# A cross-attention kernel on one Trainium2 core: units of the first attention over three slots, and one pipeline behind the first MLP

## What is computed

```python
# model 0, twice with its own weights: 16 heads of width 128, one bias key and value per head
h = layer_norm(x) * scale + offset
q, k, v = h @ wq + bq, ctx @ wk + bk, ctx @ wv + bv
k, v = concat(k, bias_k), concat(v, bias_v)
x = x + softmax(q k^T / sqrt(128)) v @ wo + bo
# then
x = x + gelu(layer_norm(x) @ w_fc1 + b_fc1) @ w_fc2 + b_fc2        # inner width 1024
# model 1: 16 heads of width 16, keys and values from ctx and from x, ctx masked
h = concat(ctx, x)
k, v = split(h @ kv_w + kv_b);  q = x @ q_w + q_b
y = softmax(mask(q k^T / 16)) v @ out_w + out_b + x
out = gelu_tanh(rmsnorm(y) * w @ mlp_w1 + b1) @ mlp_w2 + b2 + x
```

## Time and profile before

| | us |
|---|---|
| runs | 1424.93, 1425.11, 1517.13 |
| median | 1425.11 |
| the profiled execution | 1426.43 |
| its span, first to last instruction | 1424.7 |
| TensorE busy (matmul) | 1366.2 (96%) |
| DVE busy | 902.9 (63%) |
| ScalarE busy | 620.4 (44%) |
| GpSimd busy | 307.6 (22%) |
| mean granted TensorE clock | 0.983 |

### The profile page before, as it was taken

The page is one execution under the profiler, slowest core; times in us unless marked ns, Lnnn a source line. Parts: engine busy times, 40 slices in busy tenths (PEclk is TensorE's granted clock), DMA queues, the critical chain, the costliest instruction groups (busy, mean ns, idle before and its releaser), DMA issues. The chain is left out here.

```text
span 1424.7 us, 27588 instructions
## 1 busy us (share of the span) xinstructions
PE 1366.2 (96%) x11607; PEld 1219.9 (86%) x11607; DVE 902.9 (63%) x1876; ACT 620.4 (44%) x1022; POOL 307.6 (22%) x290
## 2 busy tenths in 40 slices
PE   5999999999999999999999999998898999997898
PEld 4889998999999898999999999987887877776787
DVE  4866667576666777666666666668534378886322
ACT  4633433434343564334343434346422337775421
POOL 2201011010110112011011010112863023334654
PEclk9999999999999999999999999999999999998999
DMA  5100000001100000000000000000000000002000
GB/s 154 60 31 1 30 11 21 30 1 31 30 2 31 1 31 1 30 31 1 30 1 31 31 2 30 10 22 23 1 1 9 0 2 2 2 3 64 5 30 29
DMA packets 28012, 30.53 MB, mean 21 GB/s; under 512 B 684, under 2 KB 26868, under 8 KB 27892
## 3 DMA queue, kind: packets, MB, share of 16 engines
q1 hardware_dynamic: 27668, 28.72, 6.3%
q10 hardware_dynamic: 226, 0.10, 0.0%
HBM read 26.73 MB, written 2.10 MB: 20 GB/s over the span
## 5 line engine op out<-in xcount | busy, mean ns | idle before, releaser
L334 POOL TENSOR_TENSOR WLO<-W,WHI 128x512 fp32r<-128x512 f32 x64 | 80.7, 1290 | 765.9 <-DVE WHI L728 765.9
L761 DVE STREAM_TRANSPOSE PRT<-PR 32x256 f32<-32x256 f32 x512 | 223.2, 436 | 8.4
L768 DVE TENSOR_TENSOR CLO<-bank,CHI 128x512 fp32r<-128x512 f32 x128 | 88.0, 691 | 145.6 <-ACT CHI L649 145.6
L626 ACT ACTIVATE KT<-bank,PH 128x512 f32<-128x512 f32 x128 | 88.0, 688 | 186.1 <-PE bank L171 186.1
L169 PE MATMUL bank<-WHI,CHI 128*128 128x256 f32 x576 | 167.5, 291 | 0.0
L170 PE MATMUL bank<-WLO,CHI 128*128 128x256 f32 x576 | 161.5, 280 | 0.0
L171 PE MATMUL bank<-WHI,CLO 128*128 128x256 f32 x576 | 161.0, 280 | 0.0
L169 PE MATMUL bank<-WHI,SRC_HI 128*128 128x256 f32 x504 | 146.2, 290 | 0.0
L170 PE MATMUL bank<-WLO,SRC_HI 128*128 128x256 f32 x504 | 140.9, 280 | 0.0
L171 PE MATMUL bank<-WHI,SRC_LO 128*128 128x256 f32 x504 | 140.8, 279 | 0.0
L791 DVE TENSOR_TENSOR X<-X,bank 128x512 f32<-128x512 f32 x128 | 88.0, 688 | 68.0 <-PE bank L171 67.4
(11 more groups left out here) (230 smaller groups left out, 3124.2 us busy)
## 6 DMA issues: line engine op xcount, KB each, us to landing
W<-in_wall SPq DMA_DIRECT2D x17, 1024.0 KB, 5.6
W<-in_ctx SPq DMA_DIRECT2D x4, 512.0 KB, 6.8
X<-in_x SPq DMA_DIRECT2D x4, 512.0 KB, 8.6
mlp_w<-in_w SPq DMA_DIRECT2D x2, 1024.0 KB, 9.1
out<-X SPq DMA_DIRECT2D x4, 512.0 KB, 2.9
W<-in_wall SPq DMA_DIRECT2D x1, 512.0 KB, 6.5
W<-in_wall SPq DMA_DIRECT2D x2, 256.0 KB, 8.3
W<-in_qw SPq DMA_DIRECT2D x1, 256.0 KB, 2.8
```

Of the source, the lines that this page charges most:

```text
L334: i = e.tensor_tensor(WLO[a][:, j, :, :], W[a][:, j, :, :], WHI[a][:, j, :, :].bitcast(F32), ALU.subtract)
L626: e.activation(KT[:, h, :, 0:S], PROJ[2 + h][:, :].rearrange("p (q k) -> p q k", k=S), ACT.Identity, bias=PH[:, 1, 2 * pair + h:2 * pair + ...
L761: i = e.transpose(PRT[b * S + z:b * S + z + 32, :, b * S + y:b * S + y + 32], PR[b * S + y:b * S + y + 32, :, z:z + 32])
L768: e.tensor_tensor(CLO[:, h, :], bank[3 + h][:, :], CHI[:, h, :].bitcast(F32), ALU.subtract).then_inc(c_lo, 1)
```

## The change

Three things, all in one diff of 1,500 lines.

**1. The first attention.** A unit goes over three slots. bias_at(n) becomes bias_of(u). TensorE's slot (with the last layer norm's first turn moved in front of output, and the borrowed banks of the bias turns now TB):

```diff
-                        bias, turned_before, turned_now = bias_at(n), apply_at(n - 1), apply_at(n)
+                        bias, turned_before, turned_now = bias_of(n - 1), apply_at(n - 1), apply_at(n)
...
                         keys(n)
+                        if n == 2:
+                            weighted(0)
+                        elif n > 2:
+                            output(n - 2)
...
                         queries(n)
                         values(n, 0)
                         if bias is not None:
...
+                            bias_turns(*bias, (TB[1], TB[0]), n - 1)
+                        if n == 2:
+                            output(0)
-                        weighted(n - 1)
                         values(n, 1)
...
                             norm_turn(e, norm, *turned_now, PROJ)
...
                         scores(n)
-                        output(n - 1)
+                        if n > 1:
+                            weighted(n - 1)
```

ScalarE and DVE:

```diff
                     for n in range(1, SLOTS):
-                        bias, took, now = bias_at(n), stats_at(n), apply_at(n)
+                        bias, took, before = bias_of(n - 1), stats_at(n), apply_at(n - 1)
+                        if n > 2:
+                            weighted_out(n - 2)
+                        exponential(n - 1)
+                        if before is not None:
+                            for c in range(DC):
+                                scale_chunk(e, *before, c, PROJ)
                         keys_out(n)
...
-                        weighted_out(n - 1)
                         values_out(n, 1)
...
                             norm_sqrt(e, norm, *took)
-                        exponential(n)
-                        if now is not None and now[0] < NL:
-                            scale_chunk(e, *now, 1, PROJ)
...
+                        if n >= 2:
+                            weighted_rest(n - 2)
...
                         softmax(n - 1)
...
+                        if n >= 2:
+                            settle(n - 2)
...
-                        weighted_rest(n - 1)
...
                         shifted(n)
-                        settle(n - 1)
```

**2. The way into the first MLP.** TensorE:

```diff
-                    for q in range(4):
-                        up(q)
+                    up(0)
+                    up(1)
+                    output(SLOTS - 2)
+                    up(2)
+                    up(3)
                     e.wait_ge(sub_done, SLOTS)
                     bias_turns(NL - 1, G - 1, (TB[1], None), SLOTS - 1)
                     weighted(SLOTS - 1)
+                    up(4)
                     e.wait_ge(ptb_out, NL * G)
                     norm_turn(e, norm, NL, 1, TB)
+                    up(5)
                     output(SLOTS - 1)
-                    e.wait_ge(fc2_lo, 1)
+                    up(6)
+                    up(7)
                     e.wait_ge(norm.scaled, (NL * G + 2) * DC)
                     norm_turn(e, norm, NL, 2, TB)
-                    for q in range(4, MQ + 4):
+                    e.wait_ge(fc2_lo, 1)
+                    for q in range(4):
+                        down(q)
+                    e.wait_ge(norm.scaled, (NL * G + 3) * DC)
+                    norm_turn(e, norm, NL, 3, TB)
+                    for q in range(8, MQ + 4):
```

```diff
+            def piece_of(s):
+                w, i = window(s)
+                if w == 0:
+                    if i < 4:
+                        return "v", i, 0
+                    j = i - 4
+                elif i < 2:
+                    j = i
+                elif i < 4:
+                    return ("n", w - 2, i - 2) if w >= 2 else None
+                elif i < 10:
+                    j = i - 2
+                elif i < 12:
+                    return "o", w - 1, i - 10
+                else:
+                    j = i - 4
+                g = w + 1
+                if g >= G:
+                    return None
+                if j >= 8:
+                    return "v", g * GT + j - 8, 0
+                return ("x", "kc", "q", "kx")[j // 2], g, j % 2
```

A window w is 16 steps. "x" is one of two turns of a group of x (x_hi on ScalarE, x_lo on DVE), "kc", "kx" and "q" are projections (evacuated by ScalarE), "v" a value tile (three copies on DVE, values_out), "o" two tiles of the output product (sum_y on DVE), "n" a turn of the rms-normed group (normed_out, two activations on ScalarE). TensorE waits ahead of each piece until FILL is free:

```diff
+                    def piece(s):
+                        kind, g, j = piece_of(s)
+                        e.wait_ge(*left_by(s))
...
+                            if s > LT:
+                                e.wait_ge(tl_out, s - LT)
...
+                        if s < STEPS:
+                            piece(s)
+                        elif s < STEPS + 6:
...
+                            up(s - STEPS)
+
+                    e.wait_ge(*left_by(STEPS))
+                    output(G - 1, 0)
+                    up(6)
+                    e.wait_ge(y_sum, 2 * G - 1)
+                    output(G - 1, 1)
+                    up(7)
+                    e.wait_ge(tl_out, STEPS)
+                    normed_turn(2, 0, TURN)
+                    e.wait_ge(y_sum, 2 * G)
+                    normed_turn(2, 1, FILL)
+                    for q in range(4):
+                        down(q)
+                    e.wait_ge(y_scaled, 3 * DC)
+                    for c in range(DC):
+                        normed_turn(3, c, (TURN, FILL)[c])
+                    for q in range(8, MQ + 4):
+                        if q < MQ:
+                            up(q)
+                        down(q - 4)
```

More of the change, by code:

```diff
@@ L665, in _ @@
                     queries_out(0)
-                    for c in range(DC):
-                        scale_chunk(e, 0, 1, c, PROJ)
-                    exponential(0)
                     ctx_round(2)
@@ L1402, in program, with runs @@
+            def runs(s, lag):
+                return 0 <= s - lag < STEPS
             with nc.Block() as block:
@@ L1437, in _ @@
+                    for q in range(4, 8):
+                        gelu(q)
+                    normed_out(2, 0, TURN[:, :])
+                    normed_out(2, 1, FILL[:, :])
+                    root(3)
+                    for c in range(DC):
+                        normed_out(3, c, (TURN, FILL)[c][:, :])
+                    for q in range(8, MQ):
+                        gelu(q)
                 @block.vector
                 def _(e):
-                    e.wait_ge(ob_in, 16)
-                    base(e, 0)
@@ new lines, in _, with x_lo @@
+                    e.tensor_copy(swap[:, S:P], ident[:, 0:S]).then_inc(swap_set, 1)
+                    for half in HALF:
+                        e.tensor_reduce(HM[half, :], ident[half, half].rearrange("p (h d) -> p h d", d=DH), AX_X, ALU.add)
+                    def x_lo(g, c, src):
+                        e.wait_ge(xl_hi, g * DC + c + 1)
+                        toks = slice(g * GTOK, (g + 1) * GTOK)
+                        e.tensor_tensor(SRC_LO[:, 1, c, toks], src, SRC_HI[:, 1, c, toks].bitcast(F32),
+                                        ALU.subtract).then_inc(xl_lo, 1)
@@ new lines, in _ @@
+                    for c in range(DC):
+                        x_lo(0, c, bank[3 + c][:, :])
+                    e.wait_ge(mask_in, 32)
+                    e.wait_ge(ma_set, 1)
+                    for half, row in zip(HALF, mrow):
+                        e.tensor_scalar(MA[half.start:half.start + 1, :, :], row.rearrange("p (b s) -> p b s", s=S),
+                                        0.0, MASKED, ALU.is_equal, ALU.mult).then_inc(ma_set, 1)
+                    e.wait_ge(ow_in, 16)
+                    e.tensor_copy(owh[:, :, :], owr).then_inc(owh_done, 1)
@@ L1483 @@
+                    sum_y(G - 1, 0)
+                    sum_y(G - 1, 1)
+                    normalised(3)
+                    for q in range(4, MQ):
+                        if q % FC == 4 and q > FC:
+                            add(q // FC - 1)
+                        rounded(q)
+                    add(G - 1)
 def kernel(**inputs):
```

1065 lines of the change are left out of this document (535 added, 530 removed).

## The result

The changed kernel takes 1417.46 us in the median of 5 runs (1415.68 to 1420.11), the kernel before 1424.93 to 1429.17 us in four of its five. The ratio is 0.993, 95% interval 0.9912 to 0.9947: 9 to 10 us less, clear of the spread of the runs but within the 2% that the prediction takes for the least that counts as a change. Of 50 runs of the kernel before, beside this and the later kernels, 15 took 1516.9 to 1518.9 us, as one of the three of its first row did, and are left out of the ratios, while none of 50 runs with the one-block pipeline took over 1421; parts12_alone and the kernels behind it show what is likely behind these 90 us.

What follows compares the result with a forecast made beforehand. TensorE was taken as full in the first attention and steps, losing time only at few places and two poor stages; -1.6 - 7.9 - 3.7 - 21.1 + 23.2 = -11.1 us from 1425.11 gave 1414.0 us, range 1390 to 1440.

Steps and rivals of the forecast that it cites:

- likeliest case: Whole kernel: the forecast of 1414.0 us holds, with a time between 1403 and 1425 us; chance 0.54.
- part 5: Second attention's steps: waits and visits charged for 60.7 us of matmuls moved in, +23.2 us (+6 to +50).
- part 4: Behind the steps: last MLP's matmuls fill idle time, leaving a normalisation chain that loses 2.6 us; -21.1 us (-22 to -14).
- rival A: Second attention's steps take all moved work without waits, only visits remain: 1398 us, 1393 with a free start; chance 0.18.
- Part 1: First attention: fewer switches between matmul kinds and fewer waits for queries, against a slower start; -1.6 us (-9 to +6).
- Part 2: End of the first attention: MLP matmuls between the turns fill TensorE's waits; -7.9 us (-9.5 to -4).
- Part 3: From the first MLP to step 0: most projections move into the steps, less is lost; -3.7 us (-7 to 0).
- visits: In the steps: 40 split pieces between float32 work, 0.18 us each to enter and leave, +7.2 us (4 to 12).
- port lock: In the steps: GpSimd's long operations and DVE's SBUF copies block each other on the shared port, +4 us (0 to 24).
- B: Filled steps: the single FILL bank and fixed queue orders make TensorE wait in every one, 1443 us; chance 0.15.
- C: Steps: GpSimd's additions and splits fall on DVE copies in full, +20 us instead of +4, 1430 us; chance 0.13.
- Rival D: First attention: the change there does nothing measurable; held within the forecast, with no chance of its own.

Runs made afterwards that it cites:

- parts12_alone: The changed kernel up to the end of the first MLP, followed by the second model of the kernel before: 1514.6 us.
- mlp0_order: Changed kernel with DVE's normalisation and block roundings, and GpSimd's block remainders, ahead of the second weight's split at the first attention's end: 1411.7 us.
- visits_doubled: Changed kernel with each of the 18 projections in the steps cut into two visits of three matmuls: 1416.9 us.
- short_gpsimd: Changed kernel with three of GpSimd's long operations computed on 16 of 256 columns only, the rest left uncomputed: 1410.8 us.
- root_late: Changed kernel with the third group's root split: squares behind the exponentials of steps 60 to 63, square root and normalisation later: 1406.3 us.
- combined kernel: Changed kernel with root_late, mlp0_order and ScalarE's two scalings ahead of the exponential in slot 1, all together: 1400.5 us.
- middle_filled: parts12_alone with twelve extra 256-column matmuls ahead of the scores in each of steps 28 to 35: 1474.7 us.

## Why the prediction was right

1414.0 us against 1417.5, inside the likeliest case. The likeliest mechanism, the two poor stages filled and the steps longer, is what happened, but its terms missed in both directions and evened out: part 5 by 10 us, part 4 by 8 the other way, parts 1 and 2 by 7 together. So the mechanism was right in the main, and that the total came within 3.5 us is in part luck. Two of its sums do not come out: rival A without the cost of the start is 1396 by its terms, not 1393, and the chain of part 4 leaves 2.3 us and not 2.6. Neither changes the forecast's case.

- **Part 1**: -1.6 forecast, +3.1 measured (the start's 0.4 us not counted). The start cost 3.75 in the profiled execution and 2.5 by the 63.7 of six other kernels, where 2 was forecast, and the wait of 3.9 us came out at 4.22. The slots gave 0.033 us each instead of 0.05 (14.28 for 14.31), 348.52 to 347.72 for 24 of them. The waits in the middle came out as a sum: the two of 0.84 and 1.05 us went and one of 1.25 (at 539.36) came, -0.6, where -2.2 and +1.6 had been set. What the sum did not hold at all is the bias slots: five of them took 0.20 to 0.22 more, and the last slot 0.6. In slot 30, for one, the float32 matmuls stand in three places among the split ones where they had stood in two.
- **Part 2**: -7.9 forecast, -5.6 measured. "Stretched" normalisations were priced at 1 us; they took 2.7 more than undisturbed, and TensorE waited 2.2. mlp0_order gives this back.
- **Part 3**: -3.7 forecast, -4.7 measured.
- **Part 5**: +23.2 forecast, +12.9 measured, the largest miss. The visits were mis-sized, some 4 for 40 pieces instead of 7.2 (and not by the change between kinds of matmul, as visits_doubled shows), the turns of x with the projection behind them some 4 instead of 5.5, weight roundings 0 instead of 3, the port lock about 0 instead of 4 (short_gpsimd). Against that the turns of the rms-normed groups cost 2.4 where 0.8 had been set, and the root of the last window 3.2 in the steps, where it was 2.7. The first four steps gave 1 back.
- **Part 4**: -21.1 forecast, -13.5 measured. Here the step that failed is the clock. The chain behind the steps was worked out at full clock, without the half clock that the idle time of 2.3 us in step 62 brings. With that idle time gone (root_late) the stage and the last MLP give 13.5 + 7.1 = 20.6 us, the forecast's 21.

Of the rivals, A's number (1398) is nearly what the combined kernel reaches (1400.5), by removing waits rather than by there being none. B was refuted by visits_doubled and by the filled steps of 3.5 us, C by short_gpsimd and the unstretched maxima; but four normalisations are stretched wherever they meet GpSimd, and TensorE waits for them at two places. Rival D held, even for parts 1 and 2 together: about nothing in the medians.

The prediction judged the change by the usual execution only. The largest effect of the one-block pipeline is not in the 10 us: in none of 50 runs was it some 90 us longer, as the kernel before was in 15 of 50. That those are steps at half clock is likely from the mean clock and not profiled.

## What to carry to other kernels

Price an idle time of TensorE in front of sparse float32 work by the clock that it may lose behind it, not by its length alone: here 2.3 us cost 10 with what followed, and behind 2.7 us with another 1.3 the steps took 89 us more. A stage of small matmuls that runs at the full clock in one profile can hold the half clock in another kernel with the same steps, so look at the granted clock of every run; in two kernels here, matmuls mixed into eight of the steps brought the clock back. When an operation with a table load moves into a pipeline, put it where the next table load is due anyway, and split off what needs no table.

## What the runs showed of the hardware that was not expected

- The granted clock stayed at 0.50 for 215 us (1160 to 1375) in which TensorE had no gap, in the profile of parts12_alone; its other four runs have the same time and the same mean clock (0.914 to 0.915). It rose to 1.00 within ten us when twelve matmuls of 256 columns were added per step (0.73 in the window 1250 to 1260 of middle_filled).
- The same code can be followed by half clocks of different length: behind step 62 it lasted 10.2 us in three kernels and 20.5 in two, with 24.3 to 25.9 and 29.6 to 29.8 us for the stage.
- Where four normalisations from SBUF met GpSimd's subtractions, they took 4.05, 4.63, 3.43 and 3.10 us, against 1.38 or 1.14 alone, while DVE's maxima from PSUM banks kept theirs in the steps beside the same kinds of GpSimd work (686 ns in the mean of the 13 beside long operations, 692 in the earlier trace rows).
